# A graph-attention kernel: the stores of the projected rows are issued by ScalarE instead of GpSimd

## What is computed

```
h  = x @ W                                  # 8192 x 256, fp32
s1 = h @ a[:256];  s2 = h @ a[256:]
e  = leaky_relu(s1[:, None] + s2[None, :], 0.2)
e  = where(adj > 0, e, -9e15)               # adj is 8192 x 8192 int32, very sparse
y  = x + elu(softmax(e, axis=1) @ h)
out = layernorm(y)                          # over the 256 columns
```

## Time and profile before

| | before |
|---|---|
| median of three runs | 887.17 us |
| profiled execution | 888.37 us, span 886.2 us |
| TensorE (PE) busy | 66% of the span |
| VectorE (DVE) busy | 69% |
| ScalarE (ACT) busy | 65% |
| GpSimd (POOL) busy | 69% |
| moved by DMA | 332.76 MB, mean 375 GB/s |

### The profile page before, as it was taken

One profiled execution on the slowest core, in us unless ns is written; L12 is line 12 of the kernel. 1 busy time (PEld: TensorE's weight loads), 2 busy tenths in 40 slices (PEclk: granted clock), 3 DMA queues, 4 the chain that ended last, 5 costly groups with the idle time before them and its releaser, 6 DMA issues. The chain is left out here.

```text
span 886.2 us, 10111 instructions
## 1 busy us (share of the span) xinstructions
PE 581.7 (66%) x2385; PEld 348.2 (39%) x2385; DVE 610.8 (69%) x2337; ACT 574.5 (65%) x531; POOL 608.9 (69%) x694
## 2 busy tenths in 40 slices
PE   6588985566883858757777277665766758487640
PEld 4466661232451424434434134342433424254330
DVE  4256652576996758779986577778679678487772
ACT  3035536767975968877777397575976949498410
POOL 4486426777788676788847768788777876667741
PEclk9799998877898878989889788878889879799755
DMA  8999998999999999999999889999999999899405
GB/s 332 397 405 403 377 373 329 404 407 392 403 414 417 418 415 413 415 417 416 415 417 379 345 341 417 418 351 401 381 418 420 413 397 400 339 413 409 153 23 219
DMA packets 65295, 332.76 MB, mean 375 GB/s; under 512 B 19558, under 2 KB 38215, under 8 KB 48720
## 3 DMA queue, kind: packets, MB, share of 16 engines
q1 hardware_dynamic: 36320, 289.68, 80.0%
q0 software_dynamic: 25456, 29.79, 10.1%
q10 hardware_dynamic: 3456, 12.58, 3.8%
HBM read 357.37 MB, written 17.14 MB: 423 GB/s over the span
## 5 line engine op out<-in xcount | busy, mean ns | idle before, releaser
L1453 POOL DMA_INDIRECT GATH<-haug,ids x448 | 474.8, 1060 | 130.4 <-issue 125.8
L1269 ACT ACTIVATE WORK<-ADJ 128x4096 bf16<-128x4096 int32 x128 | 461.7, 3608 | 121.1 <-PE pk L519 74.7
L519 PE MATMUL pk<-WORK,D 128*128 128x512 bf16 x1024 | 293.1, 439 | 204.4 <-ACT WORK L1269 204.0
L519 PEld LDWEIGHTS pk<-WORK,D 128*128 128x128 bf16 x1024 | 103.2, 108 | 374.5 <-ACT WORK L1269 250.2
L530 PE MATMUL acc<-GATH,diag 128*128 128x256 f32 x512 | 140.4, 423 | 45.8 <-DVE diag L808 45.6
L530 PEld LDWEIGHTS acc<-GATH,diag 128*128 128x128 f32 x512 | 106.5, 213 | 80.5 <-DVE diag L808 60.3
L1312 ACT ACTIVATE WORK<-WORK,smalls 128x1024 f32<-128x1024 int32 x16 | 18.4, 1147 | 104.1 <-DMA WORK<-in_adj_dram,smalls 71.6
L505 PE MATMUL acc<-Waug,GATH 128*128 128x258 f32 x256 | 66.1, 403 | 12.2 <-DVE GATH L735 12.2
L818 DVE SCALAR_TENSOR_TENSOR PART<-GATH,smalls,PART 128x256 f32<-128x256 f32 x128 | 62.1, 485 | 4.5
L802 DVE RECIPROCAL smalls<-smalls 128x1 f32<-128x1 f32 x64 | 10.1, 158 | 77.2 <-ACT smalls L1278 76.3
L505 PEld LDWEIGHTS acc<-Waug,GATH 128*128 128x128 f32 x256 | 48.9, 198 | 24.9 <-issue 17.0
(11 more groups left out here) (177 smaller groups left out, 715.5 us busy)
## 6 DMA issues: line engine op xcount, KB each, us to landing
ADJ<-in_adj_dram SPq DMA_DIRECT2D x128, 2048.0 KB, 13.9
haug<-GATH POOLq DMA_DIRECT2D x32, 258.0 KB, 8.4
WORK<-s_row ACTq DMA_DIRECT2D x16, 512.0 KB, 10.5
out_dram<-Y SPq DMA_DIRECT2D x32, 256.0 KB, 12.2
GATH<-haug,ids POOLq DMA_INDIRECT x448, 8.5
X<-in_x_dram SPq DMA_DIRECT2D x1, 4096.0 KB, 33.0
WORK<-in_adj_dram ACTq DMA_DIRECT2D x8, 512.0 KB, 13.7
WORK<-s_row SPq DMA_DIRECT2D x1, 4096.0 KB, 11.8
```

The lines of the kernel that those rows point to most:

```text
L519: done = nc.tensor.matmul(pk[s % PKS][:], D16[:, k, :], A16[:, q % 2, k * BW:(k + 1) * BW], start=(half == 0 and k == 0), stop=(half == 1 ...
L1269: act.activation(A16[:, q % 2, :], ADJ[:, q % 4, :], ACT.Relu, scale=HALF_SCALE if q % 2 else 1.0, accum_out=degree[:, q // 2, q % 2:q % 2 ...
L1453: pool.indirect_dma_start(out=GATH[:, r, k * DA:(k + 1) * DA], out_offset=None, in_=haug, in_offset=bass.IndirectOffsetOnAxis(ap=ids[:, t ...
```

## The change

The stores of all 32 groups leave GpSimd's program and go into ScalarE's, where each is a wait for `h_copied` and a DMA issue. Before count(q), for q from 2 to 9, ScalarE issues the stores of the groups up to PACK_AFTER[q - 2] that it has not issued yet; after count(9) it issues the stores of groups 24 to 31; then count(10) follows. The instructions of TensorE, VectorE and SyncE and their order are the same as before.

```diff
@@ ScalarE
+            def store_h(g):
+                act.wait_ge(h_copied, 2 * (g + 1))
+                act.dma_start(haug_groups[:, g:g + 1], HB[g % HBS].unsqueeze(1)).then_inc(h_stored[g % HBS], 16)
+
             for q in range(2 * EARLY):
+                if q >= 2:
+                    for g in range(PACK_AFTER[q - 3] + 1 if q >= 3 else 0, PACK_AFTER[q - 2] + 1):
+                        store_h(g)
                 count(q)
+            for g in range(PACK_AFTER[2 * EARLY - 3] + 1, G):
+                store_h(g)
             for s in range(EARLY, LAST + 1):
@@ GpSimd
-            def store_h(g):
-                pool.wait_ge(h_copied, 2 * (g + 1))
-                pool.dma_start(haug_groups[:, g:g + 1], HB[g % HBS].unsqueeze(1)).then_inc(h_stored[g % HBS], 16)
-
             for g in range(G):
                 for m in range(min(3 * g // 2, G), min(3 * (g + 1) // 2, G)):
                     sum_x(m)
-                store_h(g)
```

## The result

The changed kernel took 906.0 us (median of four runs, 900.09 to 909.3) against 887.08 us for the kernel before in the same session: a ratio of 1.020, 95% interval 1.014 to 1.026. Run once more beside other kernels it came to 905.86 us against 885.52, 1.0214 (1.0173 to 1.0254). The change costs 2%, 19 to 20 us. The profiled execution spans 905.2 us, 19.0 more than before.

The account below looks back on a forecast made before the run. Matrix loads through DMA were taken to bound the kernel, TensorE before 130 us. Held counts 7.6 us plus stores 1 us made 8.6: 897.0 on the profiled 888.37, given as 896 against the median 887.17, range 886 to 906.

Parts of the forecast that it names:

- the likeliest case: Whole kernel: counts held and stores costing about 1 us; 896 us, between 891.7 and 899, chance 0.46.
- the buffers stall too: Rival, projection: stores land later than 11.4 us, VectorE and TensorE wait, 4 to 12 us more; 899 to 907, chance 0.27.
- Held counts: Count(10) and count(11) behind stores of groups 24 to 31 release loads 14 and 15 late; 7.6 us, between 0 and 10.1.
- Stores on ScalarE's queue: Projection: stores landing late hold up VectorE's buffers; taken as 1 us by a 10.5 us landing, between 0 and 12.
- The size of the stall: Projection, upper end: 3.0 us once, 2.3 in some four further buffer rounds up to group 24, nothing behind it; 12 us.
- GpSimd's issues: Projection: GpSimd loses 32 store issues and is not waited for there; worth nothing.
- ScalarE's issues: Before counts 2 to 9: ScalarE's added issues, 0.35 us each, fall in its wait for TensorE's pack; uncovered, 24 cost 8.4 us.
- faster rival: Projection: VectorE's copies L735 shorten once GpSimd issues no stores, 5.5 us; 882 us with the loads absorbed, chance 0.06.
- Counts 2 to 9 keep their times: ScalarE in the projection: the added stores hide in waits for packs, so these counts and loads 6 to 13 do not move.
- The first gather, taken as unchanged: GpSimd behind the projection: its first gather needs the small s_row store, landed at 135.46 us, which stays; worth nothing.
- The rival Absorbed: Stretch of the gathers: slack of the counts swallows the delay, 0 to 3 us; 887 to 890, chance 0.21.
- The signs named ahead: Trace: first exponential's wait about 4 us, last copy within 1 us of 128.85, DMA share under a third 122 to 134 us.

Follow-up runs that it names:

- e11: The changed kernel, unedited, run once more beside the other kernels; 905.86 us, ratio 1.0214 against the kernel before.
- e1: The kernel before, stores still issued by GpSimd, with ScalarE waiting for the last copy of projected rows before count(10); 892.43 us, ratio 1.0069.
- e3: The changed kernel with stores of groups 24 to 27 before count(10) and count(11), 28 to 31 behind them, four buffers; 896.04 us, ratio 1.012.
- e2: The changed kernel with eight buffers for projected rows instead of four; 890.95 us, ratio 1.0063 against the kernel before.
- e10: The changed kernel with the store order of e3, four buffers, and only loads 4 to 15 split into four parts; 884.36 us, ratio 0.9986.
- e6: The changed kernel with every matrix load issued as four DMAs, 4 KB per row instead of 16 KB; 897.73 us, ratio 1.0151.
- e5: The changed kernel with each store written as 128 pieces of 2064 bytes instead of 256 pieces; 896.48 us, ratio 1.0134.
- e7: The kernel before with every matrix load issued as four DMAs, 4 KB per row instead of 16 KB; 893.21 us, ratio 1.0085.
- e12: The kernel before, stores issued by GpSimd, with only loads 4 to 15 split into four parts; 886.4 us, ratio 1.0001.
- e4: The changed kernel with the edits of both e2 and e3; 885.52 us, ratio 1.001 against the kernel before.

## Why the prediction was half right

The direction was right (slower, 0.73), and the time lies at the very end of the range (906). But the likeliest case, 896, was not what happened; it was the rival to which I gave 0.27, that the buffers stall too, priced at 899 to 907 (the 908 further on is the same sum from the profiled 888.37 us).

That 906.0 still lies in the range is luck: two of the four runs took longer (907.39 and 909.3), and the 1.0214 of e11 on 887.17 us is 906.2.

- *Held counts, taken as 7.6 us.* Right: e1 gives 6.1 (4.2 to 8.1). The mechanism is as described, DMA without work in front of a stretch that it fills, and the slack of the first exponential did not save it.
- *Stores on ScalarE's queue, taken as 1 us between 0 and 12.* This is the step that failed. e3 gives 10.6 us, and e2 and e10, which remove the stall in two different ways, bring the time back. I chose the landing time of the nearest row by bytes, 10.5 us. The stores took 16.8 to 21.1 us beside the matrix alone. The row that counted packets held the better reading, though its pair of loads, with as many packets as a store, landed in 13.7 us and not 20.2. In the page after:

```profile
q0 software_dynamic: 22896, 21.34, 7.5%
q10 hardware_dynamic: 12160, 21.04, 6.5%
```

Over the 3456 packets of before, ScalarE's queue has 12160 - 3456 = 8704 more, 272 for each of 32 stores: 256 rows of 1 KB and 16. GpSimd's queue went from 25456 (page before) to 22896, 80 for each store: 64 and 16. So GpSimd had sent four rows in one packet, if its 16 packets more are counted in the same way, and ScalarE's queue sends one. By the Trainium skill (DMA: Bandwidth & Descriptors, "Queues, rings and completion order") a DMA engine changes queue only behind a whole packet; e6 agrees, with landing from 20.2 to 7.4 us by the size of the neighbour's packets, and e5 in part. I had stated this and then let it decide nothing but a rival's chance.
- *The size of the stall.* I spread it evenly over the rounds of the buffers, as 2.3 us each. It came in two bursts (groups 12 and 13, and 25 and 26): while VectorE waits, the counts wait, the matrix loads run dry and the stores turn fast again; when the loads are back the landing time climbs once more. "Behind group 24 no load competes and nothing should stall" was wrong, since the stores that groups 25 and 26 wait for were issued right behind the copies of groups 21 and 22, from 103.7 us on, while the loads that counts 7 to 9 had released were moving; they took 12.1 to 18.9 us.
- *GpSimd's issues, ScalarE's issues, copies L735.* Right: 0.37 us an issue, hidden in the wait for the pack (3.12 us before count(9), as before), and copies of 0.68 or 0.69 us with no store from GpSimd. The faster rival is refuted.
- *Counts 2 to 9 keep their times.* Wrong from count(4) on: it starts at 75.65 us and not at 68.36, since the store in front of it waits for the copy of group 13, which the buffer holds up. Count(9) starts 7.3 us later than before. The "about 3.1" us before each count was also read too evenly: before counts 4, 5 and 7 the kernel before waited 6.05, 4.64 and 3.70 us.
- *The first gather, taken as unchanged.* Wrong: it starts at 149.50 us, 14.0 later, because s_row is stored behind the last projections. In the kernel before it was not s_row that released it, as I wrote, but VectorE's scan L744, the releaser that the earlier trace rows name; s_row had landed by about 135.2 us, 3.1 after its issue.
- *The rival Absorbed* leaned on the statement that it matters little which engine starts a DMA. For these stores beside 16 KB rows it did not hold: e3 measured 1.2%. Beside 4 KB rows it did (e10).
- *The signs named ahead.* The first exponential waited 2.48 us (about 4 forecast). The last copy of rows came 15.1 us late, where 4 was set as the mark of the stall. The three counts ran back to back, but from 145.43 us. From 122 to 134 us DMA had a share of 0.44, where under a third was forecast.

## What to carry to other kernels

When a transfer changes its issuing queue, count its packets on the new queue from the packet totals of the page, and take as its landing time at least that of a transfer with as many packets beside the same neighbours, not that of one with as many bytes. Then compare that with the time until its buffer is wanted again. When an issue with a wait is put into an engine's program, look at what stands behind it and whom that feeds: here eight stores held two counts, which held two loads, in front of a long stretch in which DMA has little time to spare.

## What the runs showed of the hardware that I had not expected

- A store of 258 KB landed in 2.4 to 21.1 us in one kernel, by what the other queue was moving; GpSimd's same store, by the count above with four rows to a packet, in 5.0 to 10.6 us.
- Loads in rows of 4 KB and not 16 KB over the whole kernel cost 0.85% (e7). Over twelve loads nothing was measured (e12), but in proportion twelve of 128 loads would cost under 0.1%, too little to be measured. The trace of e7 shows a part of it: from 200 to 820 us one issue on SyncE's queue took 1.06 us (median, up to 6.11) and not 0.33 (up to 0.65), there were four for each load, and ScalarE waited for loads 112.4 us in all and not 28.4. The share of the DMA engines there is 1.03 for 401 GB/s, and 0.99 for 400 before.
- In e2, with eight stores allowed in flight, a DMA issue on ScalarE took up to 4.46 us instead of 0.37, and in e4 up to 5.51; with four buffers no store's issue took over 0.54 (e11). What is behind it on ScalarE waits too: in e2 count(6) started at 84.81 us, right behind this issue:

```profile
80.24 4.46 ACTq L1357 DMA_DIRECT2D haug<-GATH  x1
```

That the issue waits because much is outstanding is the likely reading, from these runs and e7; no run tests it, and how much must be outstanding the runs don't say.
- Still open: the 11 us of a store's landing in e5 that do not go with its number of pieces. Some 2.7 us of them a store takes even when the matrix loads have stopped. Most of the others vanish with smaller packets beside the store (e6). One packet for each turn explains only a part of that, as worked out there.
